# Statistics of x taken tile by tile inside the counting, and the first tile normalised and transposed between the weight products

## The reference

```python
def layer0(x, edge_index, ...):        # graph attention
    x_norm = layer_norm(x, norm_g, norm_b)
    out1 = gat_conv(x_norm, src, dst, W1, a_src1, a_dst1, b1, H1=4, C1=192, N)
    out2 = gat_conv(out1, src, dst, W2, a_src2, a_dst2, b2, H2=2, C2=96, N)
    return concatenate([x, out2], axis=-1) @ Wu + bu
def gat_conv(x, src, dst, W, a_src, a_dst, bias, H, C, n):
    h = (x @ W).reshape(n, H, C)
    s_src = (h * a_src).sum(-1)
    s_dst = (h * a_dst).sum(-1)
    e = leaky_relu(s_src[src] + s_dst[dst], 0.2)
    ee = exp(e - segment_max(e, dst)[dst])
    alpha = ee / segment_sum(ee, dst)[dst]
    return segment_sum(alpha[:, :, None] * h[src], dst).reshape(n, H * C) + bias
def layer1(x, W1, b1, W2, b2, edge_index):   # graph convolution, twice, relu between
    ...
x = layernorm(x + layer0(x)); x = layernorm(x + layer1(x))
```

## Time and profile before

| what | us |
|---|---|
| median of three runs | 848.27 |
| the three runs | 843.99, 848.27, 848.43 |
| span of the profiled execution (first to last instruction) | 844.9 |
| PE busy | 794.5 (94%) |
| DVE busy | 589.5 (70%) |
| ACT busy | 295.4 (35%) |
| POOL busy | 24.7 (3%) |
| PE in the chain that ended last | 80% |
| DVE in that chain | 9% |

### The profile page before, as it was taken

One profiled execution on the slowest core, in us unless ns is written; L12 is line 12 of the kernel. 1 busy time (PEld: TensorE's weight loads), 2 busy tenths in 40 slices (PEclk: granted clock), 3 DMA queues, 4 the chain that ended last, 5 costly groups with the idle time before them and its releaser, 6 DMA issues.

```text
span 844.9 us, 11861 instructions
## 1 busy us (share of the span) xinstructions
PE 794.5 (94%) x4286; PEld 668.6 (79%) x4286; DVE 589.5 (70%) x1211; ACT 295.4 (35%) x577; POOL 24.7 (3%) x35
## 2 busy tenths in 40 slices
PE   5899999998997999999898998899979999999997
PEld 4856666665665999999666896688878889999996
DVE  2798887885999999996997998666625632212444
ACT  4446666665433344432323452122221311111000
POOL 5100000000000400000000000000000000000000
PEclk9999999999988999999898988899999999999998
DMA  9300000000003201100002300000003000000111
GB/s 316 134 2 1 1 2 2 2 1 1 0 1 122 68 1 63 63 1 1 1 1 89 115 1 2 1 1 1 1 2 130 1 1 1 1 1 19 57 56 52
DMA packets 10541, 27.77 MB, mean 33 GB/s; under 512 B 666, under 2 KB 4076, under 8 KB 9969
## 3 DMA queue, kind: packets, MB, share of 16 engines
q1 hardware_dynamic: 10480, 26.97, 9.2%
HBM read 23.09 MB, written 3.88 MB: 32 GB/s over the span
## 4 chain that ended last, share of the span: by engine, by line
PE 80%; DVE 9%; issue 7%; ACT 2%; DMA 1%; SPq 1%; DVEq 0%
PE ps L1090 77%; DVE att L639 2%; DVE att L675 2%; PE ps L1179 1%; DMA edges<-in_dst 1%; DVE out L662 1%; PE ps L1200 1%; PE ps L1233 1%; PE ps L1383 1%; DVE scrap1b L521 0%; DVE h2x L662 0%; DVE stats L726 0%; DVE mx L521 0%; PE ps L1365 0%; DVE scrap L521 0%
## 5 line engine op out<-in xcount | busy, mean ns | idle before, releaser
L1090 PE MATMUL ps<-g,att 128*128 128x193 f32 x800 | 133.6, 331 | 6.1 <-DVE att L639 6.1
L1090 PEld LDWEIGHTS ps<-g,att 128*128 128x128 f32 x800 | 132.9, 193 | 6.9 <-issue 6.7
L956 ACT ACTIVATE att<-att,ssrc 128x1250 f32<-128x1250 f32 x60 | 80.2, 1338 | 93.1 <-DVE att L675 92.9
L639 DVE SCALAR_TENSOR_TENSOR att<-att,ct 128x1250 f32<-128x1250 f32 x60 | 88.0, 1468 | 7.9 <-ACT att L956 7.7
L675 DVE SCALAR_TENSOR_TENSOR att<-uB,s 128x1250 f32<-128x1250 f32 x60 | 91.1, 1523 | 0.0
L1090 PE MATMUL ps<-wp,xT 128*128 128x388 f32 x240 | 87.5, 502 | 0.8 <-ACT xT L900 0.8
L1090 PE MATMUL ps<-yhi,ctr 128*128 128x384 f32 x200 | 67.7, 338 | 0.0
L739 DVE SCALAR_TENSOR_TENSOR ylo_a<-ps,dinv,yhi 128x384 fp32r<-128x384 f32 x32 | 19.0, 616 | 62.0 <-ACT yhi L828 62.0
L1090 PEld LDWEIGHTS ps<-wp,xT 128*128 128x128 f32 x240 | 42.5, 190 | 24.9 <-issue 1.0
L1090 PE MATMUL ps<-h2x,att 128*128 128x97 f32 x400 | 51.0, 293 | 4.2 <-DVE att L639 2.8
L828 ACT ACTIVATE yhi<-ps,dinv 128x384 fp32r<-128x384 f32 x40 | 22.2, 581 | 93.1 <-PE ps L1090 93.1
(11 more groups left out here) (243 smaller groups left out, 1441.5 us busy)
## 6 DMA issues: line engine op xcount, KB each, us to landing
uB<-u_dram SPq DMA_DIRECT2D x4, 1280.0 KB, 5.9
wux<-in_L_gnn_Wu SPq DMA_DIRECT2D x2, 2304.0 KB, 15.8
gw<-in_L_gnn_W SPq DMA_DIRECT2D x2, 2304.0 KB, 11.1
xs<-in_x SPq DMA_DIRECT2D x1, 3456.0 KB
out<-ybuf SPq DMA_DIRECT2D x9, 384.0 KB, 2.3
w<-in_L_gnn_W SPq DMA_DIRECT2D x2, 1152.0 KB, 7.0
w2x<-in_L_gnn_W SPq DMA_DIRECT2D x1, 576.0 KB, 7.5
wuo<-in_L_gnn_Wu SPq DMA_DIRECT2D x1, 576.0 KB
```

The source lines that it names most:

```text
L639: v.scalar_tensor_tensor(a, a, HUGE, ct[:, q, 0:N], ALU.min, ALU.mult).then_inc(att_ready, 1)
L956: a.activation(at_, at_, ACT.Exp, bias=ssrc[:, h, q:q + 1]).then_inc(att_exp, 1)
L1090: return t.matmul(o, lhsT, rhs, start=start, stop=stop, **kw)
```

## The change

The keys' wait of PE (`keys_out`) moves from ahead of the weight products to ahead of the third pair of groups (k == 2). DVE takes the statistics of tile 0 alone before the counting; those of tiles 2q+1 and 2q+2 follow window 0 of tile q, and their reciprocals window 2 (q = 0 to 4, tile 9 alone at the end). ACT takes tile 0's square root after the copy of group 7 (n == 7) and the others at the start of window 1; it makes the normalised rows of tile 0 (`xh0`) after the copy of group 8 and copies the transposes into `xT0` after group 10. PE transposes `xh0` after group 9. The constant product moves to bank 6, no longer waits for the last copies of the weight products, and its copy `b1w2b` is taken by DVE after window 1 of tile 0; PE waits for that copy at tile 1. DVE no longer waits for the last copies (`wp_out`) before the counting. `b1cols` and `xh0` lie in R_CT, `xT0` in R_MASK.

```diff
+            def moments(q0, q1):
+                for q in range(q0, q1):
+                    for k in range(2):
+                        last = v.bn_stats(stats[:, q, k, :], xs[:, q, k * HALF:(k + 1) * HALF])
+                last.then_inc(stats_own, 1)
+                v.wait_ge(stats_own, (q0 + 1) // 2 + 1)
+                for q in range(q0, q1):
+                    last = v.bn_aggr(mv[:, q, :], stats[:, q, :, :])
+                last.then_inc(var_ready, 1)
+            def scales(q0, q1):
+                n = (q0 + 1) // 2 + 1
+                v.wait_ge(sd_ready, n)
+                v.reciprocal(rstd[:, q0:q1], sd[:, q0:q1]).then_inc(rstd_own, 1)
+                v.wait_ge(rstd_own, n)
+                v.scalar_tensor_tensor(nmr[:, q0:q1], ...).then_inc(rstd_ready, 1)
+            def pair(q):
+                return 2 * q + 1, min(2 * q + 3, T)
             v.wait_ge(x_in, 32)
-            for q in range(T):
...
-            v.wait_ge(cst_ps, 1)
-            v.tensor_copy(b1w2b[:, :], ps[:, 1, 0:O2]).then_inc(cst_out, 1)
-            v.wait_ge(rstd_ready, 1)
-            v.wait_ge(wp_out, 2 * KD)
+            moments(0, 1)
+            scales(0, 1)
             v.wait_ge(rng_row_in, 16)
...
                     limits = window(q, r, w, limits)
+                    if q < T // 2 and w == 0:
+                        moments(*pair(q))
+                    if q < T // 2 and w == 2:
+                        scales(*pair(q))
+                    if q == 0 and w == 1:
+                        v.wait_ge(cst_ps, 1)
+                        v.tensor_copy(b1w2b[:, :], ps[:, 6, 0:O2]).then_inc(cst_out, 1)
...
                     copy(wp[:, k, 2 * hh:2 * hh + 2, :], ps[:, n % 4, 0:2 * GW]..., wp_out)
+                    if n == 7:
+                        deviations(0, 1)
+                    if n == 8:
+                        a.wait_ge(x_in, 32)
+                        a.wait_ge(rstd_ready, 1)
+                        a.activation(xh0[:, :], xs[:, 0, :], ACT.Identity, bias=nmr[:, 0:1], scale=rstd[:, 0:1]).then_inc(xh_ready, 1)
+                    if n == 10:
+                        transposed(0, xT0)
...
                 for w in range(WPT):
+                    if q < T // 2 and w == 1:
+                        deviations(2 * q + 1, min(2 * q + 3, T))
                     if w == WPT - 1 and not last:
+                        a.wait_ge(rstd_ready, q // 2 + 2)
                         fixed_place(q + 1, 1 - r)
...
             t.wait_ge(vec_out, 1)
-            t.wait_ge(keys_out, 1)
...
                 if k == 2:
+                    t.wait_ge(keys_out, 1)
                     t.wait_ge(cnt_ready, 1)
...
+                    if n == 9:
+                        t.wait_ge(rng_ready, 1)
+                        normal_transposes(0, xh0)
...
+            for j in range(NJ):
+                last = mm(ps[:, 6, 0:O2], b1cols[:, j, :], w2x[:, j, 0:O2], j == 0, j == NJ - 1)
+            last.then_inc(cst_ps, 1)
             t.wait_ge(wp_out, 2 * KD)
-            for j in range(NJ):
-                last = mm(ps[:, 1, 0:O2], b1cols[:, j, :], w2x[:, j, 0:O2], j == 0, j == NJ - 1)
-            last.then_inc(cst_ps, 1)
-            t.wait_ge(cst_out, 1)
             t.wait_ge(rng_row_in, 16)
...
+                if q > 0:
+                    t.wait_ge(cp_deg, 3 * q + 1)
+                    normal_transposes(q, xh[:, r, :])
+                if q == 1:
+                    t.wait_ge(cst_out, 1)
```

More of the change, by code:

```diff
@@ L121, in build @@
         arows = at("arows", [3 * NJ, HC], F32, R_MASK + 18176)
[L122 removed]
+        xT0 = at("xT0", [P, KD, P], F32, R_MASK)
+        b1cols = at("b1cols", [HC, NJ, P], F32, R_CT)
+        xh0 = at("xh0", [P, D], F32, R_CT + NJ * P * 4)
         mask = at("mask", [P, T, NP], BF16, R_MASK)
@@ L493, in _ @@
             v.tensor_copy(rngi[:, :], rng[:, :]).then_inc(rng_ready, 1)
-            v.wait_ge(x_in, 32)
-            for q in range(T):
[L498 to L507, removed]
-            v.wait_ge(cst_ps, 1)
-            v.tensor_copy(b1w2b[:, :], ps[:, 1, 0:O2]).then_inc(cst_out, 1)
-            v.wait_ge(rstd_ready, 1)
-            v.wait_ge(wp_out, 2 * KD)
+            def moments(q0, q1):
[12 more added lines that the diff above has]
+                v.wait_ge(rstd_own, n)
+                v.scalar_tensor_tensor(nmr[:, q0:q1], mv[:, q0:q1, 0:1].rearrange("p t a -> p (t a)"), -1.0, rstd[:, q0:q1], ALU.mult, ALU.mult).then_inc(rstd_ready, 1)
+            def pair(q):
+                return 2 * q + 1, min(2 * q + 3, T)
+            v.wait_ge(x_in, 32)
+            moments(0, 1)
+            scales(0, 1)
             v.wait_ge(rng_row_in, 16)
@@ L843, in _, with deviations, transposed @@
             last.then_inc(bcols_set, 1)
+            def deviations(q0, q1):
+                a.wait_ge(var_ready, (q0 + 1) // 2 + 1)
+                a.activation(sd[:, q0:q1], mv[:, q0:q1, 1:2], ACT.Sqrt, bias=epsc[:, 0:1]).then_inc(sd_ready, 1)
+            def transposed(q, dst):
+                for k in range(2):
+                    a.wait_ge(tp_ps, 2 * q + k + 1)
+                    for c in range(3):
+                        kk = 3 * k + c
+                        step = a.activation(dst[:, kk, :], ps[:, 4 + k, c * P:(c + 1) * P], ACT.Identity,
+                                            bias=gcol[:, KD + kk:KD + kk + 1], scale=gcol[:, kk:kk + 1])
+                    step.then_inc(tp_out, 1)
             for k in range(KD):
@@ L894, in tile @@
             def tile(q, r, behind, last):
[L896 to L902, removed]
+                if q > 0:
+                    transposed(q, xT[:, r, :, :])
                 for w in range(WPT):
+                    if q < T // 2 and w == 1:
+                        deviations(2 * q + 1, min(2 * q + 3, T))
                     if w == WPT - 1 and not last:
+                        a.wait_ge(rstd_ready, q // 2 + 2)
                         fixed_place(q + 1, 1 - r)
@@ L1124, in _, with normal_transposes @@
             t.wait_ge(vec_out, 1)
-            t.wait_ge(keys_out, 1)
             t.wait_ge(w2_in, 16)
+            def normal_transposes(q, place):
+                t.wait_ge(xh_ready, q + 1)
+                for k in range(2):
+                    for c in range(3):
+                        kk = 3 * k + c
+                        step = t.transpose(ps[:, 4 + k, c * P:(c + 1) * P], place[:, kk * P:(kk + 1) * P], identf[:, :])
+                    step.then_inc(tp_ps, 1)
             t.wait_ge(bcols_set, 1)
@@ L1214, in tile @@
                         for c in cs:
-                            step = mm(ps[:, 2 + k, 0:2 * GW], xT[:, r, c, :], wp[:, c, 2 * k:2 * k + 2, :], c == 0, c == KD - 1, skip_group_check=True)
+                            step = mm(ps[:, 2 + k, 0:2 * GW], xT0[:, c, :] if q == 0 else xT[:, r, c, :], wp[:, c, 2 * k:2 * k + 2, :], c == 0, c == KD - 1, skip_group_check=True)
                         if cs[-1] == KD - 1:
```

8 lines of the change are left out of this document (2 added, 6 removed).

## The result

The changed kernel takes 841.23 us in the median of four runs (840.3, 840.33, 842.13, 842.2), the kernel before 848.12 us (843.99 to 848.43, four runs). The ratio is 0.9929, 95% interval 0.9901 to 0.9957: faster by 0.7%. The medians lie 6.9 us apart, the means 5.9. I had forecast 845.3 with a range of 841.6 to 848.0 and given "faster by over 0.5%" a chance of 0.25.

The account below looks back on a forecast made before the run. PE was taken to bound the counting, with DVE's idle time free. 3.5 us gained ahead of tile 0's first dense product, less 0.5 lost in tiles 1 to 4, took 848.27 to 845.3 us; range 841.6 to 848.0.

Parts of the forecast that it names:

- Start of the weight products: Ahead of the counting, PE's weight products start 0.98 us earlier, at 18.75; the moved wait, reached at 24.0, costs nothing.
- ACT's piece and the wait for xh0: Before the counting, ACT's table load, square root and rows end at 33.64; PE newly waits some 1.4 us for them.
- A rule against it: A documented drain after ACT's table load would fall on PE's path: 1.3 us less gain, 846.6 us; chance 0.03.
- Between the constant product and window 0: PE's product ends at 39.89, window 0 begins at 40.15 after register loads and takes 1.44 plus 0.3 for one load.
- mark: Start of tile 0's first dense product on PE: 45.44 us before, forecast 41.9, a gain of 3.5 us.
- DVE inside tiles 1 to 4: Statistics moved into the counting exceed DVE's idle time in tiles 1 and 3: 0.5 us lost, bounds 0 and 1.03.
- The rival in which the ring makes DVE's idle time unusable: Four one-hot units limit DVE's lead, so tiles 1 to 3 lose 1.3 us each: 848.7 us; chance 0.06.
- Net at the end of tile 4: After the counting's tile 4, the 3.5 us gained less 0.5 lost leaves PE 3.0 us ahead.
- all that follows tile 4 hangs on PE's chain and shifts with it: Everything behind tile 4 was to keep the same lead, so the whole kernel gains 3.0 us.
- is no case of its own: Half-clock stretches of PE may fall on other work, 1.7 us per 3.4; they only widen the range, without their own chance.

Follow-up runs that it names:

- base_after_again: The changed kernel with a ten-bit mask on the count that two waits compare with, run once more: mean 842.1 us, ratio 0.9934 to the kernel before.
- root_sooner: The masked changed kernel with tile 0's square root behind ACT's copy of group 5, not 7, and its rows behind group 7, not 8: mean 842.0 us, ratio 0.9934.
- base_after: The changed kernel with a ten-bit mask on the count that two waits compare with: mean 842.8 us, ratio 0.9942 to the kernel before.
- spread: root_sooner with statistics of tiles 1 to 4 in DVE's square-root wait, 5 and 6 after tile 0's window 0, 7 to 9 singly in tiles 2 to 4: 841.9 us.
- const_twice: The masked changed kernel with the constant product computed twice into the same bank: mean 849.7 us, ratio 1.0025 to the kernel before.
- keys_back: The masked changed kernel with PE's wait for the keys put back ahead of the weight products: mean 845.6 us, ratio 0.9968 to the kernel before.
- base_before: The kernel before with a ten-bit mask on the count that two waits compare with: mean 848.1 us, ratio 1.0005 to the kernel before.
- keys_only: The masked kernel before with only PE's wait for the keys moved behind sixteen weight products: mean 846.2 us, ratio 0.9982 to the kernel before.
- before_const_twice: The masked kernel before with its constant product computed twice: mean 857.3 us, ratio 1.0110 to the kernel before.

## Why the prediction was right and wrong, by its own steps

**Start of the weight products.** Forecast 18.75. 18.53 in base_after_again; 20.22 in the first profile after, by the low clock. The base product was not held up (23.99, forecast 24.0). Right. (A group is four matmuls of the program and eight passes in the trace, not eight matmuls as the section on the kernel before has it; the sixteen of the forecast are four groups.)

**ACT's piece and the wait for xh0.** The chain of load, root, reciprocal and rows took what the rows of before gave. PE's idle time was 1.17 and 1.40 us, forecast 1.4, and root_sooner gave 1.0 of it back. Right.

**A rule against it.** The square root starts 0.02 us behind the table load in the new place too (33.54 behind 32.24 + 1.28). The drain of some 1380 ns that the Trainium skill, page ScalarE: Activation LUTs, section What ACT_TABLE_LOAD costs, adds is not there; the measurement decides.

**Between the constant product and window 0.** PE waits 0.17 us, forecast 0.26. Window 0 takes 1.48 us (41.74 to 43.22; 1.55 in base_after_again), forecast 1.74: most of the register load inside it, for which I took 0.3, is hidden in this window as it was in window 1. That is the term that was a little off: mark 41.52 without low clock, forecast 41.9; 3.9 us gained, forecast 3.5.

**DVE inside tiles 1 to 4.** 0.78 us lost (0.73 in the first profile after), forecast 0.5 with bounds 0 and 1.03, in tiles 1, 2 and 3. The rival in which the ring makes DVE's idle time unusable was wrong in size, right in place: the loss sits at window 1, but is 0.2 to 0.3 a tile and not 1.3. The forecast's own way of counting was wrong here: it set DVE's work against the idle time of the whole tile, by which tile 2 would lose nothing, and base_after loses 0.2 us there. That the sum came out near is in part luck.

**Net at the end of tile 4.** 3.05 us where both traces have the full clock, forecast 3.0.

**The step that failed** is the one behind that: "all that follows tile 4 hangs on PE's chain and shifts with it", and with it that the clock "is no case of its own". I had seen 0.51 in the earlier trace rows and took it as noise of both signs. But the mean granted clock of the kernel before is 0.964 and that of the changed kernel 0.970; in the profiles that is 61 to 62 us at the lower level against 51 to 54. From 404 to 532 us this alone was worth 3 us in the profiles. The forecast knew the price of such a stretch (1.7 us for 3.4) and gave it no term; a prediction of 0.3% had to name one. One reading beside the sum was also off: the 3.4 us by which the median stands above the span are not time around it. In all runs but those of spread (1.8 to 2.0) that time is 1.7 to 1.8 us, so the profiled execution took about 846.6 us and the rest is scatter. The sum, a difference, does not hang on it.

**What stays open**: why the low stretches from 410 to 500 us are long (three of four last 6.8 us) in three profiles of the old kernel and short (3.4 us, but for one in base_after_again) in all others. The time since the start is ruled out by const_twice, the idle time at 18.7 us by keys_back. Not ruled out is the place of the work against the start of the stretches themselves. From PE's row of the transposes of xs shown above (406.11 in base_before) to the first low stretch behind 410 us it is 12.7 to 12.9 us in the three profiles with the long stretches, and 13.05 us or more in the other eleven, const_twice (13.2) among them. No run moves this distance by itself, so whether it is the cause is not shown.

Of the low stretches on the first windows one thing is only suggested: of the five profiles in the old order two have a low stretch on the first windows (keys_only at 42, before_const_twice at 48), where PE has just stood idle and takes its units at DVE's pace; of the nine in the new order, in which window 0 runs without a wait, none has.

## What to carry to other kernels

Work that waits for the last product of a stage often needs only the first part of it: here a wait on the keys moved behind sixteen products and a tile's normalisation laid between them saved 3.9 us at the mark, and the price, DVE work inside a loop that another engine bounds, was a fifth of that. Lay such extra work in single pieces no longer than the idle time in front of the next unit that is waited for, and compare traces at a mark with the same clock ahead of it before a difference of the totals is explained. Where the gain sought is below 1%, the granted clock's share of the time is a term of the sum and belongs in it: a lead of 1.0 us in root_sooner was gone by 220 us, because a low stretch fell on products in place of a wait.

## What the runs showed of the hardware

The lower clock comes in stretches of 3.4, 6.8 or 10.2 us (but for the last one, which the end of the execution cuts), and ahead of the counting it was there in ten of fourteen profiles in the same program phase. PE had been busy 0.59 to 1.15 us of the 3 from 14 to 17 us in those ten and 0.98 to 1.56 in the other four, so this share alone does not tell them apart. One stretch of 3.4 us cost 1.3 us more on PE's products (root_sooner) than on a wait of PE (base_after). 2.6 us more of PE ahead of the counting made the kernel 7 to 10 us longer, for a reason that is only in part known. PE's sequencer hides most of a register load of 0.3 us under 1.5 us of products that were ready (window 0 takes 1.48 to 1.55 us, a window with the load hidden 1.44).
